# A channel-gating kernel on one Trainium2 core: new order of sums, fills and logits, and half a tile added through a scratch tile

## What is computed

```
v = group_norm(x, 32 groups)                 # mean and variance of 16 channels x 3136 pixels
r = relu(v)
r = where(max_pixels(r) - mean_pixels(r) < 0.5, 0, r)          # per channel
bb = 1 - exp(-|max_channels(r) - mean_channels(r)|)            # per pixel
y = bb * r
pooled = mean_pixels(y)
c1 = sigmoid(pooled @ W1.T)
c3 = relu(pooled @ W3.T); c3 = where(c3 < 1, 1.2, c3)
out = x + where(y < c1 * c3 * max_pixels(y), 0, y)
```

## Time and profile before

| | |
|---|---|
| median of 3 runs | 1658.56 us (1657.56 to 1660.86) |
| the profiled execution | 1656.85 us, its span 1655.1 us |
| busy: PE, DVE, ACT, POOL | 83%, 88%, 81%, 37% of the span |
| chain that ended last | ACT 35%, DVE 30%, PE 29%, issue 4%, DMA 1% |
| HBM read, written | 310.38 MB, 205.52 MB |
| granted clock, mean | 0.951 |

### The profile page before, as it was taken

How to read it: one execution, slowest core, us unless ns; L and a number is a source line. 1 busy time by engine, 2 the same in 40 slices (tenths; PEclk the granted TensorE clock), 3 DMA queues, 4 the chain that set the end, 5 groups by cost and what they waited for, 6 DMA issues and landing times.

```text
span 1655.1 us, 26670 instructions
## 1 busy us (share of the span) xinstructions
PE 1368.8 (83%) x10266; PEld 862.9 (52%) x10266; DVE 1464.5 (88%) x2192; ACT 1346.1 (81%) x2049; POOL 604.5 (37%) x414
## 2 busy tenths in 40 slices
PE   3798888888888889888889888889888888988861
PEld 1554555555555555455555455555555555545550
DVE  2599999989989999999999989999999999999997
ACT  6788988888988888888888888888898888888831
POOL 0032444432344442334442244443234444233440
PEclk8899999999999999999999999999999999999995
DMA  9349999999999999999999999999999999999973
GB/s 393 125 101 340 350 344 313 313 313 327 350 354 305 310 318 318 350 356 319 312 319 310 344 349 334 314 318 311 334 349 349 312 312 318 320 348 357 311 236 158
DMA packets 93345, 517.66 MB, mean 313 GB/s; under 512 B 10272, under 2 KB 10272, under 8 KB 93216
## 3 DMA queue, kind: packets, MB, share of 16 engines
q1 hardware_dynamic: 75360, 416.38, 62.5%
q0 software_dynamic: 17856, 99.56, 30.8%
HBM read 310.38 MB, written 205.52 MB: 312 GB/s over the span
## 4 chain that ended last, share of the span: by engine, by line
ACT 35%; DVE 30%; PE 29%; issue 4%; DMA 1%; DVEq 0%; SPq 0%; ACTq 0%
ACT junk L447 14%; DVE max_and_mean L657 13%; ACT rs L504 8%; PE ps_turn L288 8%; DVE xs L674 7%; PE ps_gate L337 6%; ACT rs L479 6%; DVE rs L674 6%; PE ps_gate L370 5%; ACT xs L504 4%; PE ps_gate L318 3%; PE ps_gate L379 2%; PE ps_gate L306 2%; ACT rows L508 1%; ACT rows L484 1%
## 5 line engine op out<-in xcount | busy, mean ns | idle before, releaser
L657 DVE TENSOR_REDUCE max_and_mean<-ps_turn 128x2 f32<-128x1024 f32 x384 | 462.4, 1218 | 34.3 <-PE ps_turn L288 32.7
L288 PE MATMUL ps_turn<-ident,xs 128*128 128x128 f32 (+1 forms) x1600 | 330.9, 290 | 147.6 <-DVE max_and_mean L657 125.6
L806 POOL TENSOR_TENSOR xs<-xs,rs 128x1568 f32<-128x1568 f32 x124 | 433.6, 3535 | 1.9 <-DVE rs L705 1.9
L797 POOL DMA_DIRECT2D xs<-in_x x124 | 111.6, 968 | 871.5 <-DVE xs L705 775.4
L447 ACT ACTIVATE junk<-xs 128x784 fp8e4<-128x784 f32 (+2 forms) x192 | 372.0, 1938 | 10.2 <-DMA xs<-in_x 2.5
L288 PEld LDWEIGHTS ps_turn<-ident,xs 128*128 128x128 f32 (+1 forms) x1600 | 191.6, 145 | 263.3 <-DVE max_and_mean L657 193.4
L288 PE MATMUL ps_turn<-ident,rs 128*128 128x128 f32 (+1 forms) x1600 | 318.3, 282 | 0.0
L674 DVE CUSTOM_DVE_ANT_0 xs<-xs,ps_gate 128x768 f32<-128x768 f32 (+1 forms) x256 | 243.7, 961 | 36.4 <-issue 36.4
L479 ACT ACTIVATE xs<-xs,shift,rstd 128x3136 f32<-128x3136 f32 x64 | 191.9, 2998 | 78.1 <-POOL shift L789 72.1
L318 PE MATMUL ps_gate<-ident,bb 128*128 128x128 f32 (+1 forms) x1600 | 229.8, 298 | 22.0 <-DVE ymax_parts L674 18.3
L318 PEld LDWEIGHTS ps_gate<-ident,bb 128*128 128x128 f32 (+1 forms) x1600 | 216.1, 211 | 51.5 <-DVE ymax_parts L674 42.2
(11 more groups left out here) (83 smaller groups left out, 1159.2 us busy)
## 6 DMA issues: line engine op xcount, KB each, us to landing
xs<-in_x SPq DMA_DIRECT2D x260, 784.0 KB, 14.0
out<-xs SPq DMA_DIRECT2D x256, 784.0 KB, 8.7
xs<-in_x POOLq DMA_DIRECT2D x124, 784.0 KB, 11.0
rs<-in_L_conv_W SPq DMA_DIRECT2D x2, 1024.0 KB, 17.7
```

The lines of the kernel that those rows point to most:

```text
L288: mm = pe.transpose(ps_turn[0:w, n % 2, b - 2 * i, P * t:P * (t + 1)], r_tile(s, t)[:, P * b:P * b + w], ident[:, :])
L657: ins = dve.tensor_reduce(max_and_mean[:, 2 * i:2 * i + 2, 0], ps_turn[:, n % 2, :, :], AX.X, ALU.max)
L806: pool.tensor_tensor(o, o, half(r_tile(s - 1, t), h), ALU.add).then_inc(added, 1)
```

## The change

Five edits, and what they move:

1. The logits. Before, four matmuls multiply the control rows with a two-column selector (`row_part`). Now PE turns the four 128 x 128 pieces of the control rows into `ps_gate`, and VectorE's copy of 8 values becomes a reduction of 48 values to 8.
2. PE's spread(s, 0) stands after the fills 5 and 6 instead of ahead of fill 5.
3. ACT's order at the end of a step: two pool sums, the last relu, gate_values 3, the other two pool sums; before it was three pool sums, gate_values 3, the relu, the fourth.
4. Half 0 of tile 1 (AGAIN) is no longer added by a transfer. SP loads x into `scratch` (128 x 1568), after the means of this step and the row means of the next sample; POOL adds it with a fifth instruction after its other four. `junk` and `rows` now lie in `scratch`; ACT waits for the addition of the step before ahead of its first square.
5. LOAD_ORDER is 2, 0, 3, 1, and SP's list has S10 and R10 later.

```
-LOAD_ORDER = (2, 0, 1, 3)
+AGAIN = 1
+LOAD_ORDER = (2, 0, 3, 1)
...
-        junk = sb("junk", [P, HW], FP8)
-        rows = sb("rows", [P, C])
+        scratch = sb("scratch", [P, HALF])
+        junk = scratch[:, 0:HW // 4].bitcast(FP8)
+        rows = scratch[:, HALF - C:HALF]
...
+                elif t == AGAIN and h == 0:
+                    sp.wait_ge(again_added, s + 1)
...
+                sp.wait_ge(means_ready, s + 2)
+                if s + 2 < B:
+                    sp.wait_ge(row_mean_ready, s + 3)
+                sp.dma_start(scratch[:, :], dram_half(x_tiles, s, AGAIN, 0)).then_inc(x_again, 16)
                 store(s, 2, 0)
...
-                store(s, 1, 0)
                 store(s, 1, 1)
...
-                reload(1, 0)
                 reload(1, 1)
+                store(s, 1, 0)
                 reload(3, 0)
                 reload(3, 1)
+                reload(1, 0)
...
-                    mm = pe.matmul(ps_control[:, :, o], control_sb[:, P * o:P * (o + 1)], row_part[:, :],
-                                   start=True, stop=True)
+                    mm = pe.transpose(ps_rows_turned[:, P * o:P * (o + 1)], control_sb[:, P * o:P * (o + 1)],
+                                      ident[:, :])
...
-                spread(s, 0)
                 turn(s, 5)
                 turn(s, 6)
+                spread(s, 0)
...
+                if s > 1:
+                    act.wait_ge(again_added, s - 1)
...
-                for t in range(3):
-                    pool_sum(s, 0, t)
-                gate_values(s, 3)
+                pool_sum(s, 0, 0)
+                pool_sum(s, 0, 1)
                 if has_next:
                     relu(s + 1, RELU_ORDER[3])
+                gate_values(s, 3)
+                pool_sum(s, 0, 2)
                 pool_sum(s, 0, 3)
...
-                dve.tensor_copy(logits[:, :], ps_logits).then_inc(logits_ready, 1)
+                dve.tensor_reduce(logits[:, :].rearrange("p (m o) -> p m o", m=2), ps_logit_parts, AX.XY, ALU.add
+                                  ).then_inc(logits_ready, 1)
...
-                        for h in range(2):
+                        for h in range(1 if t == AGAIN else 0, 2):
                             pool.dma_start(half(x_tile(s - 1, t), h), dram_half(x_tiles, s - 1, t, h),
...
+                    o = half(x_tile(s - 1, AGAIN), 0)
+                    pool.wait_ge(x_again, 16 * s)
+                    pool.tensor_tensor(o, o, scratch[:, :], ALU.add).then_inc(again_added, 1)
```

More of the change, by code:

```diff
@@ L96, in gated_sparsifier @@
         row_pick = sb("row_pick", [P, NM])
-        row_part = sb("row_part", [P, 2])
         ones = sb("ones", [P, 1])
@@ L140, in gated_sparsifier @@
         ps_group = small1[:, 0:2 * T].rearrange("p (a t) -> p a t", t=T)
-        ps_logits = small1[:, 8:8 + 2 * T]
-        ps_control = ps_logits.rearrange("p (m o) -> p m o", o=T)
+        ps_rows_turned = ps_gate[:, 1, 512:512 + C]
+        ps_logit_parts = ps_rows_turned.rearrange("p (o k m r) -> p m o k r", o=T, k=2, m=2)[:, :, :, :, 0:NS]
         ps_means = small0[:, P + 4:P + 4 + NM * MEAN_COLS].rearrange("p (i j) -> p i j", j=NM)
@@ L151, in gated_sparsifier @@
                    for p in range(XR)]
+        x_again = sem("x_again")
+        again_added = sem("again_added")
         w_loaded = [sem("w1_loaded"), sem("w3_loaded")]
@@ L562, in _ @@
                         pool_sum(s, j, t)
+            act.wait_ge(again_added, B - 1)
             copy_control(B - 1)
@@ L582, in _ @@
                               ALU.add)
-            dve.tensor_reduce(row_part[:, :], ident[:, :].rearrange("p (a m r) -> p m a r", a=2, m=2)[:, :, :, 0:NS],
-                              AX.XY, ALU.add)
             dve.tensor_reduce(row_pick[:, :], ident[:, :].rearrange("p (k r) -> p r k", k=4)[:, 0:NM, :], AX.X,
```

## The result

The changed kernel takes 1672.28 us (median of nine runs, 1663.59 to 1681.23), the one before 1658.54 beside it (1656.95 to 1660.86): ratio 1.0081, interval 1.0057 to 1.0105. It is slower, by 14 us where 8 less were forecast. The profiled execution took 1666.65, with a span of 1664.9 against 1655.1. It is 5.6 faster than the median; the profile can't say what these 5.6 are, so what follows accounts for the spans alone.

What follows compares the result with a forecast made beforehand. Waits bound the kernel, no engine being full: a loop of 49.12 us timed from the logits (moment L). 30 x (49.12 - 48.82) = 9.0, plus 0.37, minus 1.2: 8.2 off 1658.56 gives 1650.4 us, range 1633 to 1668.

Steps and rivals of the forecast that it cites:

- The logits: PE and DVE: transposes save 0.41 us, the reduction adds 0.04; net 0.37 per step, all on the path.
- Spread 0: PE: without it ahead, the 0.70 us wait for the fill goes and DVE is about 0.65 earlier.
- ACT's new order: Step's end: remaining pool sums end 0.85 us earlier, but gate_values 3 moves back 0.44, and spread 3 and the count follow.
- The gates of the last group start at 829.19 as before: DVE behind the count: the 0.65 and 0.34 us won are lost waiting for the count, so these gates don't move.
- the 0.14 a step for landings that scatter: Added to the period because reloads land 0.7 us to either side and some steps wait; gives period 48.82.
- The compute period of 48.68: Step length without transfer waits: 49.12 less 0.37 for the logits and 0.07 for the two reorders, in us.
- The transfers: DMA: 2.1 us of work freed per step; reloads allow a period of 48.65, level with the compute period.
- 49.9 - d: Shortest period the third square's reload allows; d, the queue's earlier start, lies between 0 and 2.5 us, taken as 1.25.
- tile 3 as third square: Slower rival, chance 0.16: R31 at place 15 lands after ACT's third square wants it; 1674 at d = 0.3, 1683 at 0.
- The scratch path: POOL, SP, ACT: waits cost 0, up to 0.05 us for ACT; ACT or SP waiting for the fifth addition would disprove it.
- Start and end: Outside the loop's periods: first L gains 0.37 us; the last step loses 1.58 less 0.37, taken as 1.2.
- The slower rival: Chance 0.16: tile 3's reload at place 15 lands too late for ACT's third square; 15 us more at d = 0.3.

Runs made afterwards that it cites:

- k_logits: The kernel before with the logits edit (edit 1) alone: 1648.62 us, ratio 0.9939.
- k_again: The kernel before with edits 4 and 5 alone (scratch tile, fifth addition, new load, store and reload order): 1679.55 us, ratio 1.0126.
- k_fetch: The kernel before with one store, S31, moved from place 12 to 10 of SP's list, ahead of R01 and R21: 1690.11 us, ratio 1.019.
- k_after_s31: The changed kernel with the store S31 moved from place 11 to 9, ahead of R01 and R21: 1664.30 us, ratio 1.0042 against the kernel before.
- k_after_count: The changed kernel with count_fails ahead of the keep-clock matmuls, three of which follow it: 1688.25 us, ratio 1.0174 against the kernel before.
- k_reorders: The kernel before with edits 1 to 3, without the scratch tile and with the old load order: 1649.66 us, ratio 0.9955.
- k_ls_count: The kernel before with the logits edit, count_fails ahead of the keep-clock matmuls and spread 0 behind fills 5 and 6: 1651.22 us, ratio 0.9969.
- k_l_count: The kernel before with the logits edit and count_fails ahead of the keep-clock matmuls: 1661.31 us, ratio 1.0015.
- k_s10late_count: The changed kernel with S31 at place 9, S10 last but one, and count_fails ahead of the keep-clock matmuls: 1757.58 us, ratio 1.058 against the kernel before.
- k_swapflag: The kernel before with the reload of tile 0 half 0 put ahead of the store of tile 3 half 0: 1658.39 us, ratio 1.0002.
- k_ro_count: The kernel before with edits 1 to 3 and count_fails ahead of the keep-clock matmuls, without the scratch tile: 1643.44 us, ratio 0.9905.

## Why the prediction was wrong

- **The logits: right.** Four transposes take 0.66, as forecast, the reduction 0.21 instead of 0.17. k_logits has 0.34 off the clean period (0.37 forecast).
- **Spread 0: right.** The 0.70 is gone.
- **ACT's new order: the mechanism right.** gate_values 3 became the releaser of spread 3 (1.74 of waiting), the two keep-clock matmuls and the count followed at their old lengths, and DVE waits 0.91 on average (29.2 us in 32 steps) for the 0.7 to 1.0 forecast. In a clean step the count starts 39.08 after L, 0.26 later than before (38.82); 0.44 was forecast.
- **"The gates of the last group start at 829.19 as before": this step failed.** It carried the 1.09 "issue" of the earlier trace rows over as a constant, and that gap holds a register load whose length depends on the transfers around it. I had costed edit 5 only by when the loads land. It moved S31 from place 12 to 11, so that the store lands 4.7 instead of 6.9 after the start of the flag's load, and the load grew from 0.31 to 0.91: 17.3 us more in 31 loads. That the store's fetch is the reason is a theory; that the load's length follows the store's place is shown: k_again has the loss without edits 1 to 3, k_fetch makes a larger one out of the kernel before, k_after_s31 brings the load back to 0.31. The forecast was 8.2 less, the span came out 9.8 more, and 17.3 is close to the 18.0 between them only because the other misses cancel: 4.8 for slow-clock steps, 2.3 in the last step, 0.9 for the third square and 0.4 at the end, against 6 from the compute period and 1.3 from the first L.
- **Without that step it would still have come out slower.** k_after_s31 has the load at 0.31 and takes 1664.30 where 1650.4 was forecast: about 8 of the 22 us come back, 14 stay. Its mean period is 49.29 for the 48.82 forecast, though its clean one is 48.45. Two terms were too small: the 0.14 a step for landings that scatter (the third square measured 0.33), and the slow clock, which had no term (0.42).
- **The compute period of 48.68: 0.2 too long.** Without the load's extra 0.6 the changed kernel's clean period of 49.17 would be near 48.6, and k_after_s31 has 48.45. I was 0.2 too careful there. But some steps run their keep-clock matmuls at a granted clock of 0.59 to 0.66, on the path to the count: 1.6 to 1.9 us each, in three steps of the profile and eight of k_after_s31. The forecast had nothing for that; it took 1.98 for all steps.
- **The transfers: the mechanism right, the size right by luck.** The last load is R10 now. In k_again it lands 5.96 after L in periods of 49.96, 7.74 in periods of 49.22 before: with the periods' difference out, d is about 1.0 for the 1.25 taken, and by the prediction's own 49.9 - d the transfers need 48.9, not 48.65. The third square starts later than 5.1 after L in about half of the steps, 5.1 us in sum, for 0.14 x 30 = 4.2 forecast. The two agree because the register load had made each step 0.66 longer than forecast, which gave the loads that much more time. k_after_s31 and k_after_count show the rival "tile 3 as third square" as the next bound: 9.7 and 32.9 us once VectorE is quicker.
- **The scratch path: right in time, wrong in its sign.** No row of ACT waits for the fifth addition, which takes 3.53 on POOL. SP does, in 30 steps, which the prediction named as a sign that it was wrong:

```profile
SPq L237 <- POOL xs L821: 31.2, 30, 3.1
```

S10 is issued as soon as the addition ends (824.57 in the step above). The wait costs nothing there: the reload behind S10, R30, is issued only at 827.64, when its own store has landed, and the DMA engines are busy meanwhile (share 1.03 in 825 to 829). The prediction took the time at which S10 has its turn in the queue for the time at which SP issues it.
- **Start and end.** The first L came 1.7 earlier for 0.4 forecast (k_reorders and k_ls_count have it as well, k_logits and k_l_count not, so it comes from edit 2). The last step is 3.5 longer for 1.2. The rest is PE, whose granted clock falls there. DVE in that step of the changed kernel, then PE's stretch (columns as above), then the chain:

```profile
1600.01 1.23 DVE L668 TENSOR_REDUCE max_and_mean<-ps_turn 128x2 f32<-128x1024 f32 x1 [0.93 <-PE ps_turn L297]
...
1601.71 1.23 DVE L668 TENSOR_REDUCE max_and_mean<-ps_turn 128x2 f32<-128x1024 f32 x1 [0.28 <-PE ps_turn L297]
1603.40 0.95 DVE L685 CUSTOM_DVE_ANT_0 xs<-xs,ps_gate 128x768 f32<-128x768 f32 x1 [0.46 <-PE ps_gate L327]
```

```profile
1598.00:1604.00 6.00, 6.00 (x36) 6.00 (x37) 4.29 (x5) 0.71 (x3) 6.00 (x3) 0.64 1.04 256
```

```profile
1624.87 4.53 PE ps_gate L379 x16
```

The fills and spread 0, now behind them, run in a stretch with 0.64 granted, and DVE waits 1.67 for them; before it doesn't wait there. The last products take 4.53 at 0.50 granted, before 4.03 at 0.58. With the 1.58 of the pool sum less 0.37 that makes 3.4.

The slower rival gave the right side with the wrong mechanism: tile 3 would have cost 15, and it cost 5. What the parts are worth: edits 1 to 3 together win 0.45%, no more than edit 1 alone (0.61%); edits 4 and 5 lose 1.26%, and in k_again the register load accounts for all of it. k_after_s31 has all five edits but for that store's place, and is still 0.42% slower than the kernel before.

Open: why the register load waits. The runs move the store and see the load follow, in both directions; they don't show what the two share, nor that it is the fetch, nor why k_s10late_count and k_swapflag differ. Open too is what sets where the clock falls: keep-clock matmuls moved behind the count changed it in k_l_count, and from one execution of a kernel to the next the mean granted clock differs (0.946 to 0.955 in nine of the changed kernel).

## What to carry to other kernels

A gap named "issue" is not a constant (here 1.09 before and 1.51 after in the same step): find the instruction in it, and if the sequencer reads memory there, ask what the DMA engines do at that moment before and after the change. A change to the order of transfers moves every transfer against every reader, so list what lands around each short, unhidden step. And when the compute path is shortened, price the next transfer and the clock first: here 1.5 us off the clean period (k_ro_count against before) brought 0.35 off the mean one in the profiled executions.

## What the runs showed of the hardware

- A load of one 4-byte value from SBUF into a VectorE register took 0.31 us in nearly all steps of the kernel before, and 0.65 to 1.8 in nearly all of the changed kernel, k_again and k_fetch, where the next store landed 2.6 to 4.9 us after the load's start. The vector instructions did not get longer with it: the gates take 962 ns on average against 961 before. The load's length changed with nothing but the order of the transfers (0.31 before, 1.42 in k_fetch); by which path they meet, no run shows.
- The same two keep-clock matmuls (four instructions) took 1.98 us at a granted clock of 1.00 and 2.97 to 3.34 where the clock granted over them was 0.59 to 0.66 (changed kernel, k_reorders, k_after_s31). TensorE was busy 3.94 of 4.00 us in the first stretch shown above and all of the other two.
